# Moving VectorE's edge bookkeeping into the units of a sampling loop, and an offset convolution onto column quarters

## The reference

```python
def _dcnv2(x, offset_w, offset_b, dcn_w):          # layer 0: deformable 3x3 convolution
    om = conv3x3(x, offset_w) + offset_b           # 27 channels
    off_y, off_x = om[:, :18] by tap; mask = sigmoid(om[:, 18:])
    sampled = bilinear(x, base_y + off_y, base_x + off_x) * mask
    return einsum('nckhw,ock->nohw', sampled, dcn_w)

def _forward(x, edge_index, ...):                  # layer 1 ffn: 524288 edges
    h = x_flat @ W_gat
    e = leaky_relu(a_src[src] + a_dst[dst])        # jax clamps ids to the 4096 nodes
    alpha = softmax of e over the edges of one dst
    agg = segment_sum(h[src] * alpha, dst)         # then gates of four experts
```

## Time and profile before

| what | value |
|---|---|
| median of 3 runs | 1057.0 us (1054.43 to 1057.99) |
| the profiled execution, time | 1066.97 us |
| its span | 1065.2 us |
| PE busy | 798.7 us (75%) |
| DVE (VectorE) busy | 666.0 us (63%) |
| ACT (ScalarE) busy | 364.2 us (34%) |
| POOL busy | 173.5 us (16%) |
| mean granted TensorE clock | 0.882 |
| generic_d<-generic, 2064 KB, to landing | 7.3 us |

### The profile page before, as it was taken

How to read it: one execution, slowest core, us unless ns; L and a number is a source line. 1 busy time by engine, 2 the same in 40 slices (tenths; PEclk the granted TensorE clock), 3 DMA queues, 4 the chain that set the end, 5 groups by cost and what they waited for, 6 DMA issues and landing times.

```text
span 1065.2 us, 14646 instructions
## 1 busy us (share of the span) xinstructions
PE 798.7 (75%) x4525; PEld 497.0 (47%) x4565; DVE 666.0 (63%) x1427; ACT 364.2 (34%) x559; POOL 173.5 (16%) x201
## 2 busy tenths in 40 slices
PE   4359920017998989989988788799859969766768
PEld 1212210016887868878853233344316324223757
DVE  3699778755656656647648776586564533334567
ACT  4421130004544544534452233340021625346350
POOL 5180010000000000000022000100001576760011
PEclk9589965557999999999999899999978989988689
DMA  8000000010000000000000000000010010110001
GB/s 311 0 1 1 1 0 0 2 43 39 2 1 0 0 0 0 0 0 0 0 0 1 0 0 0 2 1 0 2 42 14 6 7 7 7 7 0 3 1 79
DMA packets 11421, 15.50 MB, mean 15 GB/s; under 512 B 5568, under 2 KB 9152, under 8 KB 10992
## 3 DMA queue, kind: packets, MB, share of 16 engines
q1 hardware_dynamic: 8288, 13.87, 3.6%
q0 software_dynamic: 3088, 1.08, 1.5%
HBM read 10.35 MB, written 4.59 MB: 14 GB/s over the span
## 4 chain that ended last, share of the span: by engine, by line
PE 29%; DVE 13%; issue 6%; another core or an unknown queue 3%; ACT 3%; DVEq 1%; POOL 0%; ACTq 0%; DMA 0%; PEld 0%; PEldq 0%; POOLq 0%; SPq 0%
PE banks L1552 25%; DVE kept L1227 2%; PE banks L1904 2%; DVE wide_buf L1187 1%; PE banks L1833 1%; DVE wide_buf L1193 1%; DVE tie L1191 1%; DVE kept L1290 1%; DVE T L865 1%; DVE round_k L1289 1%; PE banks L1585 1%; ACT wide_buf L775 1%; ACT XP L788 0%; DVE shared L1398 0%
## 5 line engine op out<-in xcount | busy, mean ns | idle before, releaser
L1136 DVE TENSOR_TENSOR wide_buf<-banks,small 128x1024 f32<-128x1024 f32 x72 | 88.2, 1224 | 117.8 <-ACT small L725 117.8
L1552 PE MATMUL banks<-wide_buf 128*128 128x256 f32 (+1 forms) x720 | 144.5, 348 | 0.0
L1552 PEld LDWEIGHTS banks<-wide_buf 128*128 128x128 f32 x720 | 122.2, 194 | 12.5
L1552 PE MATMUL banks<-XP 128*128 128x32 bf16 (+1 forms) x1168 | 101.0, 227 | 35.8 <-DVE XP L990 27.4
L1552 PE MATMUL banks<-taps_w,small 128*128 128x128 f32 x618 | 92.3, 296 | 20.4 <-issue 20.4
L723 ACT ACTIVATE small<-banks,neg_x 128x512 f32<-128x512 f32 x72 | 49.5, 687 | 150.6 <-remote 64.7
L1552 PEld LDWEIGHTS banks<-taps_w,small 128*128 128x128 f32 x618 | 85.6, 203 | 31.1 <-issue 21.5
L1552 PEld LDWEIGHTS banks<-XP 128*128 128x128 bf16 (+1 forms) x1168 | 62.0, 109 | 75.0 <-issue 45.7
L588 POOL DMA_INDIRECT rows_g<-table_d,g_idx x88 | 84.9, 965 | 37.6 <-issue 32.9
L1552 PE MATMUL banks<-T,XP 128*128 (+1 forms) x128 | 69.1, 660 | 20.5 <-issue 10.6
L739 ACT COPY wide_buf<-banks 128x512 f32<-128x512 f32 (+1 forms) x87 | 49.6, 570 | 96.5 <-PE banks L1552 95.8
(11 more groups left out here) (341 smaller groups left out, 1210.8 us busy)
## 6 DMA issues: line engine op xcount, KB each, us to landing
wide_buf<-in_edges SPq DMA_DIRECT2D x2, 1536.0 KB, 14.7
generic_d<-generic SPq DMA_DIRECT2D x1, 2064.0 KB, 7.3
X<-in_x SPq DMA_DIRECT2D x4, 512.0 KB, 4.9
out_x<-X SPq DMA_DIRECT2D x4, 512.0 KB, 2.6
rows_g<-table_d,g_idx POOLq DMA_INDIRECT x88
wide_buf<-in_edges SPq DMA_DIRECT2D x2, 512.0 KB, 9.4
XP<-in_m_w SPq DMA_DIRECT2D x2, 512.0 KB, 4.8
taps_w<-in_w_dcn SPq DMA_DIRECT2D x1, 576.0 KB, 16.7
```

The costliest lines, as they stand in the source:

```text
L1136: nc.vector.tensor_tensor(near_w[s % RING], banks[:, 0:2, :], hat_x[:, h:h + 1, :].to_broadcast([P, 2, CHUNK]), ALU.mult).then_inc(w_done, 1)
L1552: return nc.tensor.matmul(o, l, r, start=start, stop=stop, **kw)
```

## The change

- Offset convolution: two pairs of images instead of four images; the four chunks of a pair go to the four 32-partition quarters of one bank, tap by tap, into a bank zeroed before; eight transposes of 128 rows; the bias is loaded four times; it starts when four chunks are padded, and ScalarE no longer waits for the keys.
- Removal leaves the place behind listing; listing comes behind hats and far test, then the codes, then num[N_FAR] and left_known, on which the engines enter sampling.
- VectorE's sampling is written out for the four images. In image 0 units 0 to 15 remove 8 groups each. Image 1 counts what is left by quarters (units 0 to 3), asks POOL (4), takes the numbers (8), lists one half of the leftovers at 10, the other at 16. Image 2 orders by position (0), counts (1 to 4), asks (5), takes the numbers and batches_known (8), and runs one twelfth (A_PARTS) of the A iterations at 10, 12, 14, 16. Then the codes of the leftovers, with PE's adds (add_left) between its images 2 and 3. Image 3 runs the other eight twelfths at 2, 4 to 16. B follows behind the last sums, then generic_made.
- POOL copies the images between the reductions and clears generic when image 2 samples. Waits for batches_known move to the batches.

```diff
-            for n in range(IMGS):
-                for h in range(2):
...
+            for m in range(PAIRS):
+                mm(ps[m][:, :], zero_b[:, 0:P], zero_b[:, :], True, False, skip_group_check=True)
+            for m in range(PAIRS):
+                pe.wait_ge(padded, 4 * (m + 1))
+                for k in range(TAPS):
+                    dy, dx = divmod(k, 3)
+                    for c in range(4):
+                        n, h = divmod(4 * m + c, 2)
+                        last = mm(ps[m][32 * c:32 * (c + 1), :], w_off[:, k, :],
+                                  XP[:, n, HROWS * h + dy:HROWS * h + dy + HROWS, dx:dx + SIDE], False, False, skip_group_check=True)
+                last.then_inc(off_ready, 1)
+            for m in range(PAIRS):
+                pe.wait_ge(off_out, m + 1)
+                for j in range(4):
+                    last = nc.tensor.transpose(ps[2 + m][:, j * P:(j + 1) * P], off_rows[:, m, j * P:(j + 1) * P], ident[:, :])
                 last.then_inc(off_turned, 1)
...
-                with dve.Fori(0, IMGS) as n:
-                    for s in range(2 * TAPS):
-                        near_unit(n, s)
+                run, _ = chained(e_chain, branch)
+                for s in range(2 * TAPS):
+                    near_unit(0, s)
+                    if s < PIECES:
+                        drop_listed(run, 8 * s)
+                for s in range(2 * TAPS):
+                    near_unit(1, s)
+                    if s < 4:
+                        count_left(run, s)
+                    elif s == 4:
+                        ask_left(run)
+                    elif s == 8:
+                        half = know_left(run)
+                    elif s == 10:
+                        list_left(half, 0)
+                    elif s == 16:
+                        list_left(half, half)
+                for s in range(2 * TAPS):
+                    near_unit(2, s)
+                    if s == 0:
+                        by_position(run)
+                    elif s < 5:
+                        count_keys(run, s - 1)
+                    elif s == 5:
+                        ask_batches(run)
+                    elif s == 8:
+                        in_a, in_b, count = know_batches(run)
+                        dve.wait_ge(made2, 7)
+                    elif s in (10, 12, 14, 16):
+                        take_front(count, (s - 10) // 2)
+                dve.wait_ge(piece_added, 3 * PIECES + 2)
+                code_left()
+                for s in range(2 * TAPS):
+                    near_unit(3, s)
+                    if s in range(2, 17, 2):
+                        take_front(count, 4 + (s - 2) // 2)
                 last_sums(IMGS - 1)
+                take_rest(in_a, in_b, count)
...
+            def take_front(count, j):
+
+                with dve.Fori(count * j, count * (j + 1)) as r:
+                    step, _ = chained(rb_chain, r * 3, True)
+                    part = keys[:, 0:FRONT_N]
                     step(nc.vector.max(top8[:, :], part))
-                    step(nc.vector.tensor_copy(generic[:, bass.ds(8 * (in_a + r), 8)], top8[:, :]))
+                    step(nc.vector.tensor_copy(generic[:, bass.ds(8 * r, 8)], top8[:, :]))
                     step(nc.vector.match_replace(part, top8[:, :], part, 0.0))
...
+            def list_left(half, first):
+
+                with dve.Fori(first, first + half) as r:
+                    step, _ = chained(r_chain, r * 3, True)
+                    step(nc.vector.max(top8[:, :], keys))
+                    step(nc.vector.tensor_copy(listed[:, bass.ds(KEPT1 + 8 * r, 8)], top8[:, :]))
+                    step(nc.vector.match_replace(keys, top8[:, :], keys, NONE))
...
+                with pe.Fori(0, IMGS - 1) as n:
+                    near_image(n)
+                add_left()
+                near_image(IMGS - 1)
...
                 for n in range(1, IMGS):
+                    pool.wait_ge(yt_ready, FILLS * n)
+                    nc.gpsimd.tensor_copy(own_img, image(T)[:, n, :]).then_inc(own_ready, 1)
+                    if n == 1:
+                        reduce_counts(2)
+                    if n == 2:
+                        reduce_counts(3)
+                        clear_generic()
```

More of the change, by code:

```diff
@@ L535, in _ @@
                         select_rows(taps, m * TAPS + first, taps, 0, m, far_sel, 1 + 6 * m + 3 * b)
-                for n in range(IMGS):
+                for n in range(1, IMGS):
                     pool.wait_ge(yt_done, 3 * SRC_T * n + 2)
@@ L910, in _ @@
                 make_keys(q)
-            run, _ = chained(e_chain)
-            dve.wait_ge(made2, 6)
-            for c in range(ECOLS // FIRST):
-                last = nc.vector.max(listed[:, 8 * c:8 * c + 8], keys[:, FIRST * c:FIRST * (c + 1)])
-            run(last)
-            for c in range(ECOLS // FIRST):
-                part = keys[:, FIRST * c:FIRST * (c + 1)]
-                last = nc.vector.match_replace(part, listed[:, 8 * c:8 * c + 8], part, NONE)
-            run(last)
+            run, run_n = chained(e_chain)
             dve.wait_ge(wa_in, WA)
@@ L991, in paired @@
                                                lane_pair[:, 0:out_.shape[2], :].unsqueeze(1).to_broadcast(grid), ALU.is_equal)
+            dve.wait_ge(made2, 6)
+            for c in range(ECOLS // FIRST):
+                last = nc.vector.max(listed[:, 8 * c:8 * c + 8], keys[:, FIRST * c:FIRST * (c + 1)])
+            run(last)
             code = code_i[:, 0:KEPT1]
@@ L1043, in _ @@
-            with dve.If(in_b > 0):
-                with dve.Fori(0, in_b) as r:
-                    step, _ = chained(rb_chain, (in_a + r) * 3, True)
-                    part = keys[:, FRONT_N:ECOLS]
+            dve.wait_ge(reduced, 1)
+            run(nc.vector.tensor_scalar(num[:, N_FAR:N_FAR + 1], counts_max[:, 1:2], FAR, None, ALU.is_gt))
+            dve.sem_inc(left_known, 1)
+            dve.wait_ge(reps_made, 1)
+            dve.wait_ge(rows_turned, 4 * IMGS)
+            branch = run_n[0]
@@ new lines, in drop_listed, with count_left @@
+            def drop_listed(run, first):
+                for c in range(first, first + 8):
+                    part = keys[:, FIRST * c:FIRST * (c + 1)]
+                    last = nc.vector.match_replace(part, listed[:, 8 * c:8 * c + 8], part, NONE)
+                if first + 8 == ECOLS // FIRST:
+                    run(last)
+            flags = generic[:, 0:ECOLS]
+            def count_left(run, q):
+                cols = slice(q * QUART, (q + 1) * QUART)
+                run(nc.vector.tensor_scalar(flags[:, cols], keys[:, cols], NONE + 1, None, ALU.is_gt))
+                run(nc.vector.tensor_reduce(rest_n[:, q:q + 1], flags[:, cols], AX_X, ALU.add))
@@ L1051, in _, with take_rest @@
-            dve.sem_inc(generic_made, 1)
+            def take_rest(in_a, in_b, count):
+                with dve.If(in_b > 0):
+                    with dve.Fori(0, in_b) as r:
+                        step, _ = chained(rb_chain, (A_PARTS * count + r) * 3, True)
+                        part = keys[:, FRONT_N:ECOLS]
+                        step(nc.vector.max(top8[:, :], part))
+                        step(nc.vector.tensor_copy(generic[:, bass.ds(8 * (in_a + r), 8)], top8[:, :]))
+                        step(nc.vector.match_replace(part, top8[:, :], part, 0.0))
+                    dve.nop()
+                dve.sem_inc(generic_made, 1)
@@ L1139, in near_unit @@
                         one_hot(n, s // 2, h)
[L1140 to L1143 removed]
+                    if s == 0 and n > 0:
+                        last_sums(n - 1)
                 def last_sums(n):
```

267 lines of the change are left out of this document (138 added, 129 removed).

## The result

The changed kernel takes 979.1 us (977.3 to 981.5, 4 runs), the kernel before in the same comparison 1056.6 (1054.4 to 1058.0, 4 runs): a ratio of **0.927 (0.925 to 0.929)**, 77.5 us less. Forecast were 988, within 968 to 1015. In what follows one run, of 1013.0 with the bucket parts two at a time, was in the slow state and is left out of its numbers.

The account below looks back on a forecast made before the run. VectorE's edge work was taken to bound the stage ahead of sampling, TensorE sampling itself. Saving 107.2 less 38.2 given back nets 69.0, from the 1057.0 median to 988.0 us; range 968 to 1015.

Parts of the forecast that it names:

- take_rest: Behind the last sums of sampling: skipping its loop costs between 0 and 8.0 us, taken as 1.5.
- Start: Ahead of sampling: first product at 138.1 instead of 245.28 us, 107.2 saved (104 to 109).
- Convolution: Offset convolution on column quarters: 18 groups take about 18 us, ending near 73 us.
- Rival B: Offset convolution: column quarters do not overlap, so 26 us of the saving are lost, 1014 us; chance 0.08.
- Image 0: Sampling's first image: removing edges, 8 pairs a unit, gives back 2.5 us.
- Image 1: Sampling's second image: counts, numbers, two leftover lists and the clock's lower level give back 17.7 us.
- Image 2: Sampling: counts, batch numbers, bucket parts and code_left at the boundary to image 3 give back 11.5 us.
- Image 3: Sampling's last image: seven buckets at 0.9 us, less 1.3, the eighth hidden, give back 5.0 us.
- a single burst E in a unit with a piece thus stalls TensorE by E - 1.9: Sampling units with a one-hot piece: VectorE work of E us in one burst stalls TensorE by E - 1.9.
- C: VectorE bounds sampling: 17 branches and loops at 2.0 us each give back 34 more, 1022 us; chance 0.10.
- D: Sampling: TensorE waits in most units and its clock stays at 1.2 GHz; slower than before, 1107 us; chance 0.04.
- no cost: Bias DMAs, bank zeroing, POOL's work, the later bucket store and moved waits delay nothing: 0 us.

## Why the prediction was right, and where it was off

The mechanism held at each step: VectorE's edge work left the path ahead of sampling, and the images took up most of it at little cost. The sum to the last product was forecast at 107.2 less 36.7 (38.2 without take_rest), 70.5; measured are 105.9 less 25.9, 80.0. The give-back was 10.8 smaller than forecast, the start 1.3 worse.

- **Start, 138.1 forecast, 139.3 measured.** Offsetting errors. Keys ended at 81.1, not 79.5, and the last hat at about 110.2, not 107.7: everything from the first norm on came 0.7 to 1.7 later, and a wait of 0.87 between the last key and the first clear was left out; the hats took their 26.1. The late keys need no cause in the change: in the second trace of the same kernel, with the same three more bias loads on POOL's queue, they ended at 79.4 and the first product came at 137.2. Flag to fill was 4.95 (4.6 to 5.2 in the eleven traces that have it), not 4; fill to product 6.9, not 9.1, for the gap of 2.0 behind the first fill did not come in this trace. Listing (11.98) and the codes were as forecast.
- **Convolution, "about 18" forecast, 15.7 measured.** (18 groups at the 1.07 of the earlier trace rows are 19.3.) Rival B is out. Its price of 26 was not measured: the run with the old convolution is not B, for its convolution goes image by image with waits between and ends at 126.5, where B's sum has 117.4. That run cost 34. It shows one term that B's sum left out: turn_rows of hats 0 and 1, 2.9 us, stands in TensorE's queue behind all the convolutions.
- **Image 0, +2.5 forecast, -0.7 measured.** The removal's units last 3.89, with VectorE never idle, as 3.76 - 1.07 + 1.29 less waits has it. But the longer units of TensorE (4.41 in the trace before) vanish in that beat, and the last of the rest is made good (4.00, 3.18): from the third product to image 1's first both traces take 64.8. The first two units take 8.2 instead of 9.0.
- **Image 1, +17.7 forecast, +17.2 measured.** Counts 0.8 for 1.0; the lists 9.2 and 7.2, for 9.7 and 6.8 with their clock terms. In the second trace the first list cost 10.5.
- **Image 2, +11.5 forecast, +6.9 measured.** Counts 2.2 for 3.1, numbers 1.3 for 2.0, the parts 1.6 in all for 2.9, the boundary with code_left 1.8 for 3.5.
- **Image 3, +5.0 forecast, +2.6 measured.** The step that failed: "a single burst E in a unit with a piece thus stalls TensorE by E - 1.9", and so seven buckets at 0.9. The rule for one burst is right: lone ones cost E - 2.05, long ones E - 1.95. It does not hold for bursts that alternate with plain units: there TensorE's catching up lies under the next burst, and a pair lasts as long as VectorE's work, 2 x 2.6 and 2.7, or 7.9: 0.4 above TensorE's 7.53.
- **take_rest, 1.5 forecast, 0 measured.**
- **Rivals C and D.** The sign given for C, a unit of over 5 in image 3, did come (5.33), but it does not part C from the forecast: the unit behind takes 2.60, and at 2.0 for a loop the pair would be near 10, not 7.9. The loops show waits of 0.25 to 0.5. Of D's low clock an image shows little: the granted clock was 0.91 over image 1, with its idle stretch of 7.7, and 0.95 to 0.98 over the others.
- **Behind sampling** "no cost" was nearly right: +1.6 from the batches' first step to the second convolution and +2.7 from there to the experts' hidden layer, in every kernel with the moved edge work. The kernel with the convolution part alone showed the second too (31.9 against 29.2) and not the first, whose cause is open. The second is TensorE's clock: here is that stretch, before and after.

```profile
782.29:811.49 29.20, 24.20 (x120) 14.69 (x121) 20.68 (x40) 6.19 (x10) 0.00 (x0) 0.85 0.15 39
```

```profile
704.33:736.19 31.86, 27.00 (x120) 17.07 (x121) 20.67 (x40) 6.19 (x10) 0.00 (x0) 0.77 0.14 35
```

  The same 120 matmul records take 27.0 instead of 24.2, at a granted clock of 0.77 instead of 0.85; the other engines' work is the same. Both traces of the kernel before have 0.85 there, all twelve others 0.77, with the old convolution or the new. What lowers it is open.

- **The sum.** Before the step to the median, 998 was forecast for a run like the profiled one; the changed kernel's has 975.5 of span and 1.8 around it, 977.3, so 20.7 less. Of these 11.0 are the points up to the norm (10.8 given back less, take_rest 1.5, the start -1.3), 14.7 the gathers and experts, and -4.9 and -0.3 the other stages, all rounded. Taking the 69.0 off the median of 1057.0 instead of the profiled 1067.0 allowed for 10 of the 14.7, without knowing where this surplus sat; so 988.0 was only 8.9 too high.

## What to carry to other kernels

Before work is put into an engine's idle time in a pipelined loop, read per place how long the others can go on without it: here 2 us in a lone unit, some 1.2 in each of two neighbouring units, 2.3 where every second unit is plain, and more at an image's end (lists of 9.9 lost 9.2 in the middle and 7.2 near the end). Cut the work to that size and alternate; a burst twice as long cost nine to twelve times as much (3.5 to 4.9 against 0.4), for the excess counts in full and the clock can fall on top. And when two parts of a change shorten chains that join, cost them together: the convolution was worth 5 alone and 34 beside the move.

## What the runs showed of the hardware that was not expected

- fp32 matmuls of 128x32 by 128x512 on four column quarters of one bank, with a weight load each, run at 0.87 us for four over 18 groups in a row.
- From the flag to TensorE's first work inside the branch pass 4.6 to 5.2 us in eleven traces; VectorE takes about 4 from its last straight code (one trace read). The loops of one iteration inside sampling add only 0.25 to 0.5.
- TensorE's clock was low behind idle stretches of 2.6 and 3.3 us in image 3 of the run with parts two at a time, which cost 0.8 to 1.5 us each time, and not low behind one of 3.28 in the same image.
- In the stretch from the second convolution to the experts' hidden layer TensorE's granted clock was 0.85 in both traces of the kernel before and 0.77 in the twelve of the other kernels, which cost 2.7 us.
- A stage of indirect gathers and experts took 176 to 196 us in the traces, alike within each comparison on one chip, whatever the kernel; TensorE's records in it lengthened with it, and the other engines' did not.
